# Attention of a graph transformer: context and projection in two buffers each, column sums in halves, and another order of TensorE's transposes and products and of VectorE's work

## The reference, cut to what matters

```python
x = x + _L0_gnn_ref(_layernorm(x), adj, ...)   # attention, 4 heads of 32, with an output layer norm (gamma, beta)
x = x + _L0_ffn_ref(_layernorm(x), ...)        # mixture of 8 experts, top 2
x = x + _L1_gnn_ref(_layernorm(x), adj, ...)   # attention, 8 heads of 16
x = x + _L1_ffn_ref(_layernorm(x), ...)        # 30 recurrent steps
# one attention, per graph and head:
s = where(adj == 0, -1e9, q @ k.T * scale); w = softmax(s); out = (w @ v) @ Wo + bo
# the first one then: (out - mean) * rsqrt(var + eps) * gamma + beta
```

## Time and profile before

| What | us |
|---|---|
| median of 3 runs (2990.65 to 2991.92) | 2991.47 |
| the profiled execution, its own time | 2996.56 |
| its span | 2994.7 |
| PE busy (92% of the span) | 2751.5 |
| VectorE busy (84%) | 2517.4 |
| ScalarE busy (72%) | 2154.1 |
| GpSimd busy (57%) | 1693.7 |
| first attention, from 25 to 485 us: PE, VectorE, ScalarE, GpSimd busy | 372.06, 323.44, 277.12, 249.67 |
| mixture, from 485 to 990 us: the same | 493.52, 424.61, 220.18, 174.38 |
| second attention, from 990 to 1620 us: the same | 560.56, 418.91, 363.46, 94.52 |
| recurrent block, from 1620 us to the end: the same | 1322.66, 1342.20, 1292.09, 1170.20 |

### The profile page before, as it was taken

The page is one execution under the profiler, slowest core; times in us unless marked ns, Lnnn a source line. Parts: engine busy times, 40 slices in busy tenths (PEclk is TensorE's granted clock), DMA queues, the critical chain, the costliest instruction groups (busy, mean ns, idle before and its releaser), DMA issues. The chain is left out here.

```text
span 2994.7 us, 69062 instructions
## 1 busy us (share of the span) xinstructions
PE 2751.5 (92%) x20318; PEld 1803.7 (60%) x20447; DVE 2517.4 (84%) x6998; ACT 2154.1 (72%) x4096; POOL 1693.7 (57%) x1120
## 2 busy tenths in 40 slices
PE   5888886999999799999995699999999999999999
PEld 3555555888888466666663555555555555555556
DVE  4777775888888566666666799999999999999999
ACT  4666652444444466666663799999999999999994
POOL 2565654333333211111112599999999988888882
PEclk9999997999999899999997699999999999999999
DMA  5000000000000000000000155555555555555555
GB/s 144 22 21 20 19 8 15 1 0 0 0 0 0 26 16 14 14 14 14 14 8 4 57 199 198 198 198 198 198 198 198 198 198 198 198 198 198 198 198 170
DMA packets 132585, 281.78 MB, mean 94 GB/s; under 512 B 11760, under 2 KB 69152, under 8 KB 132512
## 3 DMA queue, kind: packets, MB, share of 16 engines
q1 hardware_dynamic: 115616, 272.44, 26.7%
q10 hardware_dynamic: 16896, 8.39, 1.0%
HBM read 270.49 MB, written 10.29 MB: 94 GB/s over the span
## 5 line engine op out<-in xcount | busy, mean ns | idle before, releaser
L1321 POOL TENSOR_TENSOR d_g<-d_g,d_rb 128x1024 f32<-128x1024 f32 x464 | 1084.1, 2371 | 127.2 <-DMA d_rb<-d_rstd_rows 112.0
L1400 DVE BATCH_NORM_STATS2 d_stats<-d_p_gt 128x6 f32<-128x256 f32 x1920 | 942.8, 647 | 23.3 <-PE d_p_gt L1536 23.2
L1522 PE MATMUL d_p_y<-d_g,d_w_main 128*128 128x512 f32 x1856 | 952.6, 595 | 0.0
L1393 DVE SCALAR_TENSOR_TENSOR d_th<-d_th,d_p_y 128x512 f32<-128x512 f32 x960 | 863.7, 900 | 4.1 <-ACT d_th L1577 4.1
L1536 PEld LDWEIGHTS d_p_gt<-ident,d_g 128*128 128x128 f32 x3840 | 450.9, 142 | 541.1 <-ACT d_g L1581 385.8
L1581 ACT ACTIVATE d_g<-d_th,d_bias 128x512 f32<-128x512 f32 x928 | 666.6, 718 | 12.0 <-DVE d_th L1393 0.9
L1577 ACT ACTIVATE d_th<-d_p_y,d_bias 128x512 f32<-128x512 f32 x928 | 625.2, 674 | 0.3 <-PE d_p_y L1522 0.3
L1536 PE MATMUL d_p_gt<-ident,d_g 128*128 128x128 f32 x3840 | 592.3, 278 | 0.1
L223 POOL TENSOR_TENSOR a_rstd<-a_var,minus_half 128x4 f32<-128x4 f32 x64 | 66.0, 1032 | 559.7 <-DVE a_var L316 557.9
L1050 DVE SCALAR_TENSOR_TENSOR x_sb<-m_p_y,m_combine,x_sb 128x128 f32 (+1 forms) x1024 | 312.0, 344 | 68.5 <-PE m_p_y L1092 52.5
L337 DVE TENSOR_REDUCE a_row_max<-a_p_s 128x4 f32<-128x512 f32 x384 | 238.2, 683 | 132.0 <-PE a_p_s L461 132.0
(11 more groups left out here) (217 smaller groups left out, 4062.6 us busy)
## 6 DMA issues: line engine op xcount, KB each, us to landing
d_rb<-d_rstd_rows SPq DMA_DIRECT2D x464, 512.0 KB, 5.4
a_adj_in<-in_adj_dram SPq DMA_DIRECT2D x64, 256.0 KB, 2.8
out_dram<-d_out_sb ACTq DMA_DIRECT2D x32, 256.0 KB, 2.5
d_rstd_rows<-d_rstd_row SPq DMA_DIRECT2D x116, 16.0 KB, 1.4
m_w_sb<-in_L_ffn_w_dram SPq DMA_DIRECT2D x2, 512.0 KB
x_sb<-in_x_dram SPq DMA_DIRECT2D x1, 256.0 KB, 2.9
a_w_raw<-in_L_gnn_Wq_dram SPq DMA_DIRECT2D x2, 64.0 KB, 2.2
a_w_raw<-in_L_gnn_Wk_dram SPq DMA_DIRECT2D x2, 64.0 KB, 2.1
```

Source lines behind the costliest of these rows:

```text
L1321: nc.gpsimd.tensor_tensor(g[:, c, :], g[:, c, :], rb[:, buf, :], ALU.mult).then_inc(s_gs, 1)
L1393: nc.vector.scalar_tensor_tensor(out=th[:, b, cols(u)], in0=th[:, b, cols(u)], scalar=0.01, in1=p_y[:, b, cols(u)], op0=ALU.mult, op1=ALU. ...
L1400: ins = nc.vector.bn_stats(stats[:, q % 2, (j * CT + t) // 2].rearrange("p a s -> p (a s)"), p_gt[:, t * P:(t + 2) * P].rearrange("p (a c) ...
L1522: nc.tensor.matmul(p_y[:, c % 2, cols(u)], w_main[:], g[:, c, cols(u)], start=True, stop=True).then_inc(s_y, 1)
```

## The change

context_t and proj get two buffers, chosen by the parity of the quad. VectorE's first body does maxima and take_maxima back to back, then the reciprocal and the context product, then the statistics of x, all four normalisations of the projection in one go, the offset, and the statistics of the projection last. The context product waits for the projection one quad further back. sum_prob works on two graphs at a time (256 columns), in two calls. In PE's first body the transpose of the maxima goes ahead of the transposes of x, and transpose 1 of prob goes to p_z, where it waits for v, instead of p_x, where it waited for the context. In PE's second body the projection is split around the transpose of the maxima, the sums of the second part come ahead of the context products, and transpose 1 goes behind the scores of the other part. ScalarE's copy of the projection waits one quad further back. GpSimd's and SyncE's queues are as before.

```diff
-        context_t = sb("context_t", [P, QUAD])
+        context_t = sb("context_t", [P, 2, QUAD])
         if normed:
-            proj = sb("proj", [P, QG, P])
+            proj = sb("proj", [P, 2, QG, P])
             stats_o = sb("stats_o", [P, QG // 2, 2, 3])
             var_o = sb("var_o", [P, QG])
...
                     dve.wait_ge(s_den, PARTS * (k + 1))
                     nc.vector.reciprocal(rden[:], p_y[:]).then_inc(s_rden, 1)
 
-                def normalise_context(k):
+                def normalise_context(k, par):
                     dve.wait_ge(s_pv, PARTS * (k + 1))
                     dve.wait_ge(s_rden, k + 1)
-                    wait(dve, s_o, k)
-                    nc.vector.tensor_tensor(context_t[:], p_x[:], rden[:], ALU.mult).then_inc(s_ctx, 1)
+                    wait(dve, s_o, k - 1)
+                    nc.vector.tensor_tensor(context_t[:, par], p_x[:], rden[:], ALU.mult).then_inc(s_ctx, 1)
 
...
 
-                def stats_projection(k):
+                def stats_projection(k, par):
                     dve.wait_ge(s_fin, k + 1)
+                    wait(dve, s_fn, k)
                     for g in range(0, QG, 2):
                         last = nc.vector.bn_stats(stats_o[:, g // 2].rearrange("p a s -> p (a s)"),
-                                                  proj[:, g:g + 2, :].rearrange("p a c -> p c a"))
+                                                  proj[:, par, g:g + 2, :].rearrange("p a c -> p c a"))
                     last.then_inc(s_fln, 1)
                     dve.wait_ge(s_fln, k + 1)
                     nc.vector.tensor_scalar(var_o[:].rearrange("p (g a) -> p g a", a=2), stats_o[:, :, :, 2],
                                             1.0 / P, EPS, ALU.mult, ALU.add).then_inc(s_fvar, 1)
 
-                def normalise_projection(k, half):
-                    if half == 0:
-                        dve.wait_ge(s_frstd, k + 1)
-                        wait(dve, s_done, k)
-                    for g in (2 * half, 2 * half + 1):
-                        last = nc.vector.tensor_scalar(proj_n[:, g, :], proj[:, g, :], stats_o[:, g // 2, g % 2, 1:2],
+                def normalise_projection(k, par):
+                    dve.wait_ge(s_frstd, k + 1)
+                    wait(dve, s_done, k)
+                    for g in range(QG):
+                        last = nc.vector.tensor_scalar(proj_n[:, g, :], proj[:, par, g, :], stats_o[:, g // 2, g % 2, 1:2],
                                                        rstd_o[:, g:g + 1], ALU.subtract, ALU.mult)
-                    if half:
-                        last.then_inc(s_fn, 1)
+                    last.then_inc(s_fn, 1)
 
                 def first_body(k, par):
...
                         maxima(k)
-                    if live(k - 3):
-                        normalise_projection(k - 3, 0)
-                    if live(k):
                         take_maxima(k, p_w)
-                    if live(k - 3):
-                        normalise_projection(k - 3, 1)
                     if live(k - 1):
                         invert_sums(k - 1)
-                        normalise_context(k - 1)
+                        normalise_context(k - 1, 1 - par)
                     if live(k + 3):
                         stats_x(k + 3)
-                    if live(k - 2):
-                        stats_projection(k - 2)
+                    if live(k - 3):
+                        normalise_projection(k - 3, 1 - par)
                     if live(k + 3):
                         offset_x(k + 3)
+                    if live(k - 2):
+                        stats_projection(k - 2, par)
 
...
                         invert_sums(k - 1)
-                        normalise_context(k - 1)
+                        normalise_context(k - 1, 1 - par)
                     if live(k):
                         maxima(2 * k + 1)
...
 
-                def sum_prob(part):
+                def sum_prob(part, half):
+                    columns, graphs = slice(2 * half * P, 2 * (half + 1) * P), slice(2 * half, 2 * half + 2)
                     for t in range(4):
-                        last = nc.tensor.matmul(p_y[tile(t), :], ones[:, part, :], prob_t[:, t],
-                                                start=part == 0, stop=part == PARTS - 1)
-                    last.then_inc(s_den, 1)
+                        last = nc.tensor.matmul(p_y[tile(t), columns], ones[:, part, :], prob_t[:, t, graphs],
+                                                start=part == 0 and half == 0, stop=part == PARTS - 1 and half == 1)
+                    if half:
+                        last.then_inc(s_den, 1)
 
...
 
-                def project(k, bank):
-                    pe.wait_ge(s_ctx, k + 1)
-                    nc.tensor.matmul(bank[:], ones_bf[:], bias_rows[:], start=True, stop=False)
-                    for g in range(QG):
-                        last = nc.tensor.matmul(bank[:, graph(g)], context_t[:, graph(g)], w_o[:], start=False,
+                def project(k, par, bank, graphs=range(QG)):
+                    if 0 in graphs:
+                        pe.wait_ge(s_ctx, k + 1)
+                        nc.tensor.matmul(bank[:], ones_bf[:], bias_rows[:], start=True, stop=False)
+                    for g in graphs:
+                        last = nc.tensor.matmul(bank[:, graph(g)], context_t[:, par, graph(g)], w_o[:], start=False,
                                                 stop=g == QG - 1)
...
                         pe.wait_ge(s_ptc, 4 * (k - 1) + 1)
                         transpose_prob(k - 1, 2, p_w)
-                        if live(k):
-                            pe.wait_ge(s_v, k + 1)
+                        pe.wait_ge(s_ptc, 4 * (k - 1) + 2)
                         transpose_prob(k - 1, 3, p_z)
                     if live(k + 1):
-                        if live(k - 1):
-                            pe.wait_ge(s_ptc, 4 * (k - 1) + 2)
+                        wait(pe, s_ctx, k - 1)
                         product_q(k + 1, 1 - par, p_x)
                     if live(k - 1):
                         pe.wait_ge(s_ptc, 4 * k)
                         if live(k - 3):
                             pe.wait_ge(s_fin, k - 2)
-                        sum_prob(0)
+                        sum_prob(0, 0)
+                        sum_prob(0, 1)
+                    if live(k):
+                        transpose_maxima(k, p_w)
                     if live(k + 2):
                         transpose_x(k + 2, p_z)
-                    if live(k):
-                        transpose_maxima(k, p_w)
                     if live(k - 1):
...
@@ -571,13 +572,11 @@
                             pe.wait_ge(s_rden, k)
                         else:
                             pe.wait_ge(s_fin, k - 2)
-                        project(k - 2, p_y)
-                    if live(k):
-                        if live(k - 1):
-                            pe.wait_ge(s_ctx, k)
-                        else:
-                            pe.wait_ge(s_q, k + 2)
-                        transpose_prob(k, 1, p_x)
+                        project(k - 2, par, p_y)
+                    if live(k):
+                        if live(k + 1):
+                            pe.wait_ge(s_v, k + 2)
+                        transpose_prob(k, 1, p_z)
 
...
                         else:
                             pe.wait_ge(s_fin, k - 2)
-                        project(k - 2, p_z)
+                        project(k - 2, par, p_z, (0, 1))
                     if live(k - 1):
                         pe.wait_ge(s_ptc, 4 * n)
                     if live(k):
                         transpose_maxima(n, p_w)
+                    if live(k - 2):
+                        project(k - 2, par, p_z, (2, 3))
                     if live(k - 1):
-                        pe.wait_ge(s_v, k)
-                        context_product(1 - par, 1, (0, 1))
+                        sum_prob(1, 0)
                     if live(k):
                         shift_scores(n)
                     if live(k - 1):
-                        context_product(1 - par, 1, (2, 3))
-                        sum_prob(1)
+                        sum_prob(1, 1)
+                        pe.wait_ge(s_v, k)
+                        context_product(1 - par, 1, range(QG))
                     if live(k + 1):
                         if live(k):
                             pe.wait_ge(s_mtc, n + 1)
@@ -621,15 +622,15 @@
                         else:
                             pe.wait_ge(s_v, k + 1)
                         transpose_prob(n, 0, p_z)
+
+                    n = 2 * k + 1
+                    if live(k):
+                        scores(k, par, 1)
                         if live(k + 1):
                             pe.wait_ge(s_xtc, k + 2)
                         else:
-                            pe.wait_ge(s_mtc, n + 1)
-                        transpose_prob(n, 1, p_w)
-
-                    n = 2 * k + 1
```

(32 more changed lines are left out.)

## The result

The changed kernel takes 3051.86 us (median of 4 runs, 3050.07 to 3053.40) against 2991.69 us before: ratio 1.0201, 95% interval 1.0183 to 1.0218, so 60 us slower. The forecast was 3066, 75 us slower. The measured time lies inside the range of 3037 to 3089, at the lower edge of what the forecast had as its own (3052 to 3078), and nearer to the rival "the clock stays" (3044) than to 3066.

A forecast was written before the change was run, and what follows sets the result against it. The first attention was taken as bound by a chain through several engines, the second by PE. Terms of 78 + 22 - 4 - 21 = +75 us gave 3072 against the profiled execution, 3066 for the median, range 3037 to 3089.

The forecast's parts named there:

- the clock stays: Rival, first attention: GpSimd's chain holds VectorE, but PE's clock falls behind the sums or not at all; +53, 3044 us, chance 0.18.
- What bounds: First attention bound by a chain through several engines, 13.01 us a body, second by PE; freed waits worth about 1.4 us.
- GpSimd's three products come between normalisation and rstd: First attention: the offset waits for rstd behind GpSimd's products, about 5.3 us; body 16.0 instead of 13.01 us, +78 us.
- The clock: First attention: PE idles about 4.6 us before the sums, its clock halves; 0.85 us a body, +22 us, bounds 0 and +25.
- the first rival: First attention: PE's clock falls behind the sums or not at all, so costs nothing; 3044 us, chance 0.18.
- Ends of the first attention: Bodies 0 to 2 and 29 to 34 lose the wait for the old context in some: -4 us, bounds 0 and -8.
- Second attention: PE's waits before transpose 1 and the second transpose of maxima go: 0.69 us a body, -21 us, bounds -8 and -25.
- Sums in halves: Both attentions: sixteen matmuls of 256 columns for eight of 512 cost 0, bounds 0 and +0.1 us each.
- the rival of dear halves: Rival, both attentions: each matmul has its own price, so a halved sum costs 0.27 us more; +24, 3090 us, chance 0.06.
- Sum: Whole kernel: the terms 78 + 22 - 4 - 21 give +75 us, a forecast of 3066 us.
- The other side: Rival, first attention: GpSimd has rstd within 1 us of the normalisation's end, PE binds; 2935 us, chance 0.04.

The follow-up runs named there:

- e2: Changed kernel with VectorE's old order in the first attention, buffers, PE's new order and halved sums kept: ratio 0.9746 to the kernel before, body 11.42 us.
- e3: Changed kernel with 14 extra unread matmuls filling PE's idle stretch ahead of the sums in the first attention: ratio 1.0168 to the kernel before, body 16.08 us.
- e1: Changed kernel with GpSimd computing rstd(k+3) ahead of its three products: ratio 0.9848 to the kernel before, first attention's body 12.50 us.
- e6: Changed kernel without GpSimd's beta sum (result differs, run for time alone): ratio 1.0046 to the kernel before, first attention's body 14.79 us.
- e5: Kernel before with only VectorE's new order in the first attention, one buffer each, PE's old order, whole sums: ratio 1.0654, body 20.27 us.
- e7: Changed kernel with PE's body of the second attention as before: ratio 1.0283 to the kernel before, second attention 18.27 us a body.
- e8: Changed kernel with rstd(k+3) ahead of GpSimd's three products, and these waiting for the offset: ratio 0.9758 to the kernel before, body 11.43 us.
- e9: e2 with each sum in one piece of 512 columns again: ratio 0.9742 to the kernel before, first attention's body 11.41 us.
- e11: e8 with each sum in one piece of 512 columns again: ratio 0.9742 to the kernel before, first attention's body 11.43 us.

## Why the prediction was right, step by step

- *What bounds.* Right. The second buffers and PE's order do free the first attention: with VectorE's old order the body is 11.42 us (e2), the 1.4 us less that the step gave and a little more.
- *GpSimd's three products come between normalisation and rstd.* Right in place, and in the size of the wait: it was put at 5.3 us and is 5.18. The chain without the clock was put at 16.0 and is 15.99 (e3, 25 bodies), 77 us in all for the 78 taken. That it hits so closely is in part luck: the bodies are of two kinds, and the sum describes one of them, which takes 15.72. Its roundings added 0.3 us (0.1 between the third product and rstd, for one, where the trace has no gap), and the other kind takes 16.28, for delays on VectorE that the sum doesn't have. Undoing the queue order (e1), VectorE's order (e2) or one link (e6) takes the time off, and the order alone on the kernel before brings it (e5).
- *The clock.* The mechanism is right, the size was too large: 0.85 us a body was taken, e3 and the changed kernel give 0.46 over the same 25 bodies, that is 11.5 us for 22. Two things fell short. The sums were slow, wholly or in part, in 20 of the 26 bodies, not in all; in the other six they took 1.07 us, as the first rival has it. And where they were, part of the delay was hidden: in every other body the split of the maxima ended later anyway (4.2 us behind the offset's end, and 3.8 in the others, in e3 as in the changed kernel), so a slow sum there cost 0.58 us (16.85 for 16.27) and not 0.85 (16.57 for 15.72). This, and the 1 us of the step before, are the difference between 100 us forecast for the bodies and 88.3 measured.
- *Ends of the first attention.* -4 was taken, -6.1 measured.
- *Second attention.* -21 was taken, -22.3 measured between its marks, and some 3.8 more in its start (the stretch ahead of it is 574.0 us in e7 and 570.2 in the changed kernel); both waits went, the one for take_v stayed, as said.
- *Sums in halves.* 0 was taken, with 0.1 us each as the bound. In the second attention the whole sums save 0.13 to 0.18 us a body of two sums, inside that bound; the rival of dear halves, at 0.27 us a sum, is out.
- *Sum.* 78 + 22 - 4 - 21 = +75 against +56.4 between the two profiled executions: 11.7 us less in the bodies, 2.1 in the ends, 1.3 in the second attention, 4.0 ahead of it, and 0.4 back. The medians differ by 60.2. The error of the forecast is thus mostly the term of the clock, about 10 us too large.
- *The other side* needed rstd to be ready within 1 us of the normalisation. e1 makes just that true. It forecast 11.8 us a body and 2935 us; e1 has 12.50 and 2949.8. The step that failed there is the assumption that VectorE's small instructions cost beside GpSimd's products what they cost alone.

## What to carry to other kernels

Before an instruction is moved in one engine's queue, read the queue of the engine that it feeds and that feeds its neighbours: here a result needed at once stood last in GpSimd's queue, behind three products that the move had pulled off their cover. If a wait appears for a tiny instruction (1.04 us of work, 5.2 us of wait), look at what is queued ahead of it and not at its own cost; moving that one instruction up turned +2.0% into -1.5%. The fastest of the runs, e2, e8, e9 and e11 at 0.974 to 0.976, keep the buffers and PE's new order and differ in how GpSimd's products are kept off the path, and in whole or halved sums; of their bodies of 11.41 to 11.43 us PE is busy 11.1 (e2).

## What the runs showed of the hardware

- VectorE's small instructions stand still beside some of GpSimd's. In e1 the offset, 0.16 us alone, took 1.23 and ended 0.02 us behind GpSimd's product; the variance, 0.17 alone, took 0.64 and 0.72 (e8) and did the same. When the offset did not overlap a product it took 0.16 again (e8). The Trainium skill (SBUF — State Buffer, Who interferes with whom) states that a VectorE instruction with two SBUF inputs contends with GpSimd instructions that read SBUF, and one in a mode with two ports contends with GpSimd, and that the one that issues later is blocked for the whole of the other. The offset has two such inputs and agrees. The variance has one. That it is in such a mode is what the page would make of it; no run here tested that.
- Beside GpSimd's mask (1.94 us) the delay depends on where in the mask the instruction starts, and it is not always for the whole of the mask. L342 took 0.17 us when it started 1.3 us into the mask (e3, above) and 0.41 when it started 1.56 into it. L344, which has two inputs in SBUF, took 0.17 when it started 1.5 us into the mask (the kernel before and the changed one), and 0.50 when it started 0.13 us into it, but there it ended 1.3 us ahead of the mask (e1, rows below). The page's rule doesn't account for that; what in the mask holds VectorE at its start and its end stays open.

```profile
234.80 1.94 POOL L226 TENSOR_SCALAR a_mask<-a_adj_in 128x512 bf16<-128x512 int32 x1
...
234.93 0.50 DVE L344 SCALAR_TENSOR_TENSOR a_split<-a_row_max,a_split 128x16 bf16<-128x16 f32 x1
```

- What the half clock costs differs with the order of the instructions: 0.46 us a body in the changed kernel, 2.6 in e5. Products that nobody reads, 3.2 us of them in a stretch of 4.5, kept the clock at 0.99 (e3) and brought 0.3 us a body net.
